# Moving the evacuation of the values' PSUM bank from ScalarE to VectorE in a fused attention and feed-forward kernel

## The reference

```python
x = L0_attn_x                                   # (4, 1024, 256) fp32
xn = _layernorm(x)
x = x + attn(xn, Wq, Wkv, Wout, bout) + ffn(xn, w_gate, w_up, w_down)

# attn: 16 heads of 16; the keys are also the values
q, kv = split(xn @ Wq), split(xn @ Wkv)         # (b * heads, n, 16)
q, kv = rotary(q) * SCALE, rotary(kv)
attn = softmax(einsum('bmd,bnd->bmn', q, kv))
out = einsum('bij,bjd->bid', attn, kv)          # then merged, @ Wout + bout
# ffn: silu(gate) * up, dequantised int weights, hidden size 768
```

## Time and profile before

| | us |
|---|---|
| median of 3 runs | 955.86 |
| the three runs | 951.65, 955.86, 958.96 |
| the profiled execution | 953.67 |
| its span, first to last instruction | 951.9 |
| L755, the copy: 32 instructions | 19.1 in sum, 0.597 each |
| L937, the reductions: 512 instructions | 592.2 in sum, 1.215 each |

### The profile page before, as it was taken

How to read it: one execution, slowest core, us unless ns; L and a number is a source line. 1 busy time by engine, 2 the same in 40 slices (tenths; PEclk the granted TensorE clock), 3 DMA queues, 4 the chain that set the end, 5 groups by cost and what they waited for, 6 DMA issues and landing times.

```text
span 951.9 us, 21905 instructions
## 1 busy us (share of the span) xinstructions
PE 840.3 (88%) x6962; PEld 318.5 (33%) x6962; DVE 787.4 (83%) x987; ACT 675.8 (71%) x1280; POOL 159.6 (17%) x376
## 2 busy tenths in 40 slices
PE   1879999999769999999999999999999999999973
PEld 1445554555412222222232322222222232222223
DVE  5877787877699999999998989998898998899502
ACT  2244443324228999999989988988998998998960
POOL 1113333113300110001011121111121111121110
PEclk9989999999959999999999999999999999999997
DMA  9011001112100111101112111111111121111114
GB/s 310 21 44 45 23 26 40 44 44 71 51 18 25 24 26 41 31 23 24 33 52 55 41 41 46 49 52 50 43 40 46 46 55 48 44 40 46 36 41 144
DMA packets 58810, 47.07 MB, mean 49 GB/s; under 512 B 18425, under 2 KB 48889, under 8 KB 58769
## 3 DMA queue, kind: packets, MB, share of 16 engines
q1 hardware_dynamic: 58768, 46.55, 17.4%
HBM read 28.77 MB, written 17.04 MB: 48 GB/s over the span
## 4 chain that ended last, share of the span: by engine, by line
PE 43%; issue 15%; DVE 14%; DMA 7%; POOL 7%; SPq 7%; ACT 6%; DVEq 1%; POOLq 0%; ACTq 0%
PE ps L588 16%; DVE negmax L937 8%; PE ps L605 7%; PE ps L571 7%; DMA arena<-inv_d 6%; ACT arena L741 5%; PE ps L519 5%; POOL hl L1016 5%; PE ps L477 4%; SPq L324 3%; PE ps L613 3%; SPq L354 2%; DVE arena L852 2%; POOL arena L1070 1%; SPq L350 1%
## 5 line engine op out<-in xcount | busy, mean ns | idle before, releaser
L937 DVE TENSOR_REDUCE negmax<-ps 128x2 f32<-128x1024 f32 x512 | 592.2, 1215 | 46.1 <-PE ps L605 45.3
L741 ACT ACTIVATE arena<-ps 128x512 f32<-128x512 f32 x1024 | 555.9, 597 | 47.0 <-PE ps L571 36.3
L588 PE MATMUL ps<-arena 128*32 128x256 f32 (+1 forms) x3664 | 316.2, 417 | 0.3 <-ACT arena L741 0.2
L605 PE MATMUL ps<-ks,qs 48*128 48x512 f16 x1024 | 204.5, 396 | 19.9 <-DVE negmax L937 17.9
L571 PE MATMUL ps<-qs,ks 51*128 51x512 f16 x1024 | 198.2, 383 | 23.4 <-ACT arena L741 21.4
L605 PEld LDWEIGHTS ps<-ks,qs 48*128 48x128 f16 x1024 | 49.4, 93 | 204.2 <-issue 129.5
L588 PEld LDWEIGHTS ps<-arena 128*32 128x32 f32 x3664 | 72.4, 108 | 115.7 <-issue 105.8
L691 ACT ACTIVATE gact<-ps 128x512 f32<-128x512 f32 x48 | 28.4, 592 | 95.8 <-PE ps L497 95.8
L571 PEld LDWEIGHTS ps<-qs,ks 51*128 51x128 f16 x1024 | 49.4, 93 | 126.4 <-ACT arena L741 88.6
L477 PE MATMUL ps<-wqkv,arena 128*128 128x512 f32 x128 | 59.3, 618 | 6.5 <-issue 6.5
L1016 POOL TENSOR_TENSOR hl<-hid,hh 128x512 f16<-128x512 f32 x48 | 54.3, 1164 | 33.1 <-ACT hh L697 33.1
(11 more groups left out here) (71 smaller groups left out, 533.1 us busy)
## 6 DMA issues: line engine op xcount, KB each, us to landing
parts_d<-arena SPq DMA_DIRECT2D x64, 128.0 KB
x_all<-x_dram SPq DMA_DIRECT2D x8, 512.0 KB, 8.2
qs<-parts_d SPq DMA_DIRECT2D x64, 64.0 KB, 1.9
ks<-parts_d SPq DMA_DIRECT2D x64, 64.0 KB, 1.8
o_d<-arena SPq DMA_DIRECT2D x128, 32.0 KB
arena<-o_d SPq DMA_DIRECT2D x24, 128.0 KB
arena<-inv_d SPq DMA_DIRECT2D x48, 64.0 KB
out_dram<-arena SPq DMA_DIRECT2D x24, 128.0 KB, 1.7
```

The source lines that it names most:

```text
L588: mm = pe.matmul(ps[32 * j:32 * j + 32, 7, cols], vstage[pl % 2][:, j % 2, kt, :], probs[PER_STEP * (kt % PBUF) + j][:, cols], start=(kt = ...
L605: mm = pe.matmul(ps[:, 2 * h + a, :], qs[ring][top:top + PROD, kt * P:(kt + 1) * P], ks[ring][top:top + PROD, h * CHUNK:(h + 1) * CHUNK], ...
L741: act.activation(probs[PER_STEP * (kt % PBUF) + j], ps[:, score_bank(ls, j), :], ACT.Exp).then_inc(exp_done, 1)
L937: dve.tensor_reduce(negmax[pl % 2][:, h, :, kt], ps[:, 2 * h:2 * h + 2, :], AX.X, ALU.max, negate=True).then_inc(max_done, 1)
```

## The change

The copy moves from ACT's program to DVE's, with the same waits and the same semaphore. On DVE it stands ahead of the first reduction of a pair's second step, that is ahead of the reduction for half step 2. The last pair's copy, after the loops, moves likewise.

```diff
@@ exps, on ACT
                     act.activation(probs[PER_STEP * (kt % PBUF) + j], ps[:, score_bank(ls, j), :], ACT.Exp
                                    ).then_inc(exp_done, 1)
-                    if j == 0 and kt == COPY_O_AT and not (isinstance(p, int) and p == 0):
-                        copy_o(p - 1, ls // STEPS - 1, turn)
...
-            def copy_o(p, slot, turn):
-
-                act.wait_ge(pv_done, STEPS * (p + 1))
-                if not (isinstance(p, int) and p < 2):
-                    act.wait_ge(o_stored[slot % 2], 16 * (PER_STEP + 1) * (turn * (RING // 2) + slot // 2))
-                act.activation(osb[slot % 2], ps[:, 7, :], ACT.Copy).then_inc(o_copied, 1)
...
-            copy_o(PAIRS - 1, RING - 1, TURNS)
@@ DVE
+            def copy_o(p, slot, turn):
+
+                dve.wait_ge(pv_done, STEPS * (p + 1))
+                if not (isinstance(p, int) and p < 2):
+                    dve.wait_ge(o_stored[slot % 2], 16 * (PER_STEP + 1) * (turn * (RING // 2) + slot // 2))
+                dve.tensor_copy(osb[slot % 2], ps[:, 7, :]).then_inc(o_copied, 1)
@@ step, on DVE
                 q = ls // STEPS
+                if ls % STEPS == COPY_O_AT and (q or not isinstance(turn, int)):
+                    copy_o(turn * RING + q - 1, q - 1, turn)
                 if not last_turn or m < RING * STEPS:
                     maxima(turn, m, 0)
                     maxima(turn, m, 1)
@@ after the last step
+            copy_o(PAIRS - 1, RING - 1, TURNS)
             invert(PAIRS - 1, PAIRS - 1)
```

## The result

The changed kernel takes 957.32 us in the median of 20 runs (954.54 to 962.04), the kernel before 953.43 in the median of 20 (951.29 to 958.96). The ratio is 1.0038, with a 95% interval of 1.0026 to 1.0049: slower by 0.38%, some 3.6 us. The forecast was 3.2 us more than before. (The forecast time of 959.1 us stood on the median of the first three runs, 955.86; on the median of twenty, 953.43, the same 3.2 gives 956.6.)

A forecast was written before the change was run, and what follows sets the result against it. Both ACT and DVE were on the path, with DVE's row of reductions setting the pace in pairs without a tile. Terms 2.1 + 1.0 + 0.1 = 3.2 us, put on the median 955.86, gave 959.1 us; range 951 to 969.

The forecast's parts named there:

- The price of the copy: Each of 32 copies on DVE takes 0.68 us, holding DVE for 0.61; ends 0.35 and 0.70 kept.
- The wait for the values: DVE's wait before its copy for the old pair's values costs nothing, as DVE is still reducing then.
- Pairs without a tile: Nine copies: 0.61 us against 0.40 of DVE room leaves 0.21 lost at half step 14; 2.1 us in sum.
- Pairs with a tile up to 820: DVE's idle time absorbs the copy and the projection still waits for GpSimd; 0.1 us in sum.
- The late ones: In four late pairs with a tile GpSimd is ready early, so the projection waits for DVE's copy; 0.9 us together.
- last copy: After the loop, DVE's copy takes 0.68 in place of 0.60 on the path to the last stores; 0.1 us.
- The signs of being wrong: A pair with a tile up to 820 growing by over 0.2 us, or one without a tile getting shorter.
- The full price: Rival, chance 0.14: PE never regains the delay, each copy costs all 0.61; 18.9 us, 974.8, slower by 2.0%.
- ACT as the path: Rival, chance 0.09: ACT's relief shortens pairs with and without a tile; -11 us, 944.9, faster by 1.2%.

The follow-up runs named there:

- e5: Changed kernel with DVE's copy cut to 256 of 512 columns; ratio 0.998 to the kernel before, -1.9 us.
- e3: Against the kernel before, DVE copies only in the nine pairs without a tile, ACT in all others and at the end; ratio 1.0013.
- e1: Kernel before with ACT's copy cut from 512 columns to 16, nothing added on DVE; ratio 0.9962, -3.6 us.
- e2: Kernel before, ACT still copying, plus a spare 512-column DVE copy before the reduction of half step 2 in 30 pairs; ratio 1.0024, +2.3 us.
- e0: The changed kernel unaltered, run again beside the kernel before; ratio 1.0036, median 957.65 us.
- e4: Against the kernel before, ACT copies in the nine pairs without a tile, DVE in the 22 with one and at the end; ratio 1.0024.
- e7: Kernel before with ACT's copy behind the first exponential of half step 3, not 2, in pairs without a tile; ratio 0.999.
- e9: Kernel before with ACT's copy one half step later in pairs without a tile, measured a second time; ratio 0.998.
- e6: Changed kernel plus a spare 512-column DVE copy before the reduction of half step 2; ratio 1.0162 to the kernel before, +15.4 us.

## Why the prediction was right, point by point

**The price of the copy.** 0.68 us and DVE held for 0.61; measured 680 ns and 0.60. The rows that read from `ps` were the right neighbours and the casts from SBUF the wrong ones. The rule of the Trainium skill (VectorE: DVE Perf Modes, "Why PSUM operands drop a tier") is borne out by this: 680 ns for 512 and 416 ns for 256 elements (e5) is 1.03 ns an element, no doubled rate.

**The wait for the values.** Predicted to cost nothing; in 30 of 32 copies DVE had no idle time before it, and the two others are the last ones, where DVE waits anyway.

**Pairs without a tile.** Predicted: +0.21 us a pair, half step 14 as the place that holds it, 2.1 us in sum. Measured: +0.18 (19.41 for 19.23), PE's wait of 0.21 at half step 14, and distances 2 to 10 together 1.3 us longer in the changed kernel and in e3. The term was 0.8 too large. More than half of this is the first distance with a copy, which got shorter (19.21 for 19.44) where I had it 0.25 longer. There, before the rhythm has settled, ACT's relief does count: this distance is 19.03 in e1, where only ACT is relieved, and 19.43 in e2, where only DVE is burdened. The other 0.3 are the eight pairs behind it, 0.19 each in the mean where my terms give 0.23. e1 and e2 show the two halves of the step apart: 0.4 us won by ACT's relief when nothing is put on DVE, and 0.18 lost by DVE's burden when ACT is not relieved. With both, the loss is the same as with DVE's alone. I had said that ACT's relief would be of no use, and in the settled pairs that is what e2 beside the change shows; e1 shows that it is so only because DVE's copy takes the same room.

**One detail of it was wrong.** PE's wait at half step 4 was to be put down to DVE, and the idle time before half step 15 to stay 0.36. The wait is still ACT's (0.26), and the idle time is 0.44. In the kernel before, half step 14's matmuls came late enough to stretch a row of five reductions to 5.76 us; now it is 5.68, and the 0.08 show up behind it. Neither changes the sum.

**Pairs with a tile up to 820.** Predicted: 0.1 us in all, because the copy's end plus 0.05 stays under GpSimd's product. With the measured 0.13 it does not: in about half of these pairs the projection follows the copy as if it waited for it. The price is small. The projection's waits, without the three long ones of over 0.9 us, add up to 3.9 us over pairs 11 to 26 in e0 and e4 (4.2 in after), 3.3 in before, and 3.0 to 3.8 in e1 to e3, e5 and e7 to e9. e4's middle distances are 0.24 longer than e3's, and kernels that don't touch these pairs scatter by more (328.08 in before to 328.78 in e1). So a loss of up to about 0.6 us is likely and not shown.

**The late ones.** Predicted: 0.9 us, with L613 waiting for the copy. Measured: L613 waits for it, and the last four distances together grow by 1.3 us in after and e0 and by 1.5 in e4. In e3, where ACT copies in them, they grow by 0.3, all of it in one where the projection waited 0.26 us for GpSimd. One mis-sized piece is the time from the copy's end to L613. I took the 0.05 us that lie between GpSimd's product and L613; from DVE's copy it is 849.04 - (848.23 + 0.68) = 0.13 here; in e0 and e4 it is 0.13 in three of the four and 0.06 in the last. That makes some 0.25 of the 0.4 that the term was too small. The other piece may be DVE's burden by itself, to which e2 points in two of these pairs; how the two add up was not measured.

**The sum.** 2.1 + 0.1 + 0.9 + 0.1 = 3.2 against 3.6 us: the first term 0.8 too large and the late one 0.4 too small. These two measure 1.3 and 1.3 us; the remaining 1.0 is located nowhere with certainty. It lies within what the middle pairs, the end part with its last copy (0.1 predicted, not resolved) and the granted clock scatter. So the agreement of the total is better than that of its terms, and in part luck.

**The signs of being wrong that I had named.** Both came, by their letter. A distance of a pair without a tile got shorter, the second (19.21 for 19.44 us, and 19.22 and 19.21 in e0 and e3): there the mechanism was another, as told above. And pairs with a tile up to 820 grew by over 0.2 us in the one profile: the nineteenth by 1.70, with a fall of the clock told of below, the twenty-second by 0.38, with GpSimd late (0.62 us of wait), and the twenty-first by 0.25. The twenty-second has 0.08 in e0 and 0.04 in e4, so it is scatter. The twenty-first is 20.28 to 20.41 us in after, e0 and e4, and 20.08 to 20.22 in before, e1 to e3, e5 and e7 to e9, so part of this growth is real.

**The rivals.** The full price fell with e2 (+2.3 for 30 copies, not +18), and e6 shows where it begins in the plain pairs: with the second copy. ACT as the path fell with e1, in the form that gives every pair a gain; in the nine plain pairs it was half true.

## What to carry to other kernels

When an instruction moves between two busy engines, ask at its place, not over the span, how much idle time the receiver has before the next thing that someone waits for: DVE had 0.40 us there, and the copy held it for 0.60, so 0.2 was lost, though ACT was free for 0.49 more. What the donor gives back counts only up to the receiver's next tight place. And of the moved instruction's result, look for the readers that were served just in time: its later end cost at most a tenth or so in each pair in which the reader waited about as long for GpSimd and a DMA, and some 0.3 us in each of the four in which it did not.

## What the runs showed of the hardware that I had not expected

One pair of the changed kernel took 22.81 us where it takes 21.11 before, and again 22.77 in e0 and 22.85 in e2. In these three it is the nineteenth distance; e9, in which ACT copies, has such a pair three times, the fifteenth (22.84), the nineteenth (22.45) and the twenty-third (22.65). So it is nothing of the changed kernel alone. By stretch, in after and then in before (columns as in the earlier trace rows; the third number from the end is the granted clock):

```profile
640.00:644.00 4.00, 2.80 (x22) 1.08 (x14) 3.75 (x4) 2.04 (x4) 0.72 (x1) 1.00 0.38 105
644.00:648.00 4.00, 3.52 (x20) 0.56 (x22) 2.45 (x2) 2.34 (x5) 0.72 (x1) 0.60 0.19 46
648.00:652.00 4.00, 4.00 (x48) 1.20 (x46) 2.94 (x3) 3.76 (x8) 0.00 (x0) 0.97 0.00 0
```

```profile
644.00:648.00 4.00, 3.75 (x36) 1.07 (x38) 3.07 (x3) 3.70 (x9) 0.73 (x1) 1.00 0.17 36
```

The granted clock fell to 0.60 in the mean of 4 us, so for most of them to the lower level of 1.2 GHz, and a whole block of values took 1.93 us where it takes 1.07. Ahead of it PE had waited 1.18 us for GpSimd, one of the long waits that every fourth pair has; in the kernel before it was 0.97 there:

```profile
642.53 1.13 PE L613 MATMUL ps<-wo,arena 128*128 128x256 f32 x4 [1.18 <-POOL arena L1070]
```

```profile
642.10 1.13 PE L613 MATMUL ps<-wo,arena 128*128 128x256 f32 x4 [0.97 <-POOL arena L1070]
```

But e1 waited 1.34 us at this place and e4 1.12, and both kept their clock, while e0 lost it behind 1.12 and e9 behind 1.15, 1.10 and 1.04. So a long wait goes with the drop and doesn't suffice for it; what else belongs to it stays open. A drop costs some 1.3 to 1.7 us.

The mean clock of an execution goes with its time: of the 20 runs of the changed kernel the three with a mean clock of 0.973 took 954.5 to 954.8 us, the one with 0.966 took 962.0. It does not say where the clock was low, since the end part differs too (0.74 over 925 to 951 us in before and after, 0.67 in e0). But it allows a comparison at equal clock, of the 31 runs of the changed kernel (with e0) and the 85 of the kernel before beside the experiments. At 0.973 the means are 954.4 us (4 runs) and 952.1 (36), at 0.971 they are 956.3 (6) and 953.6 (14), at 0.970 they are 958.1 (6) and 955.4 (23), and at 0.969 they are 957.8 (14) and 954.3 (8). So 2.2 to 3.5 us of the loss are there at equal clock, and most of the loss is not a matter of the clock. The changed kernel reached 0.973 less often, in 4 of 31 runs against 36 of 85; but so did e7 to e9 together, in 1 of 36, and they are not slower than before. Whether the copy's place on DVE has a part in it, and the last few tenths of the 3.6 us come from it, these runs can't tell.
